# Band attention with a small network on one core: V transposed by DMA instead of TensorE, and GpSimd's low halves issued piece by piece

## What is computed

```
xn = layernorm(x)
Q, K, V = xn Wq + bq, xn Wk + bk, xn Wv + bv            # per head: 1024 x 64
scores = Q K^T where |i - j| <= 64, and 0.0 elsewhere   # zeros stay in the softmax
attention = softmax(scores) V Wo + bo
s = xn Win + bin;  h = relu(s * W1 + b1);  g = sum(h * W2) + b2   # 64 units, 16 inner each
out = x + attention + g Wout + bout
```

## Time and profile before

| | us |
|---|---|
| median of 3 runs | 2201.57 |
| lowest, highest | 2192.87, 2208.58 |
| the profiled execution | 2183.65 |
| its span | 2181.9 |
| mean granted TensorE clock (1.00 is 2.4 GHz) | 0.961 |

### The profile page before, as it was taken

One profiled execution on the slowest core, in us unless ns is written; L12 is line 12 of the kernel. 1 busy time (PEld: TensorE's weight loads), 2 busy tenths in 40 slices (PEclk: granted clock), 3 DMA queues, 4 the chain that ended last, 5 costly groups with the idle time before them and its releaser, 6 DMA issues.

```text
span 2181.9 us, 42699 instructions
## 1 busy us (share of the span) xinstructions
PE 1958.2 (90%) x14211; PEld 1107.1 (51%) x14211; DVE 1824.1 (84%) x4579; ACT 1480.3 (68%) x3961; POOL 1517.1 (70%) x2272
## 2 busy tenths in 40 slices
PE   8768799998999989998899998998989998999985
PEld 4435455554555545554455554554555554555543
DVE  7779687898789887998889888889888898888775
ACT  5767667775767756766667775775757775777753
POOL 3655657877588757867578775686748876687764
PEclk8988899999999999999999999999999999999997
DMA  4454453755366543754356654375444755365534
GB/s 124 118 134 98 97 116 84 174 112 112 69 128 160 101 93 83 164 123 99 81 103 150 136 101 102 80 186 107 87 93 103 173 102 108 78 141 112 117 78 106
DMA packets 610427, 247.04 MB, mean 113 GB/s; under 512 B 547336, under 2 KB 559648, under 8 KB 610208
## 3 DMA queue, kind: packets, MB, share of 16 engines
q1 hardware_dynamic: 610160, 244.30, 50.9%
q10 hardware_dynamic: 48, 0.01, 0.0%
HBM read 84.84 MB, written 25.17 MB: 50 GB/s over the span
## 4 chain that ended last, share of the span: by engine, by line
PE 34%; DVE 26%; POOL 15%; ACT 13%; issue 7%; DMA 5%; SPq 1%; DVEq 0%; ACTq 0%; POOLq 0%
PE ps L1143 17%; POOL probs L388 8%; ACT probs L532 7%; POOL p_lo L401 6%; DVE acc L888 5%; PE ps L1199 5%; PE ps L1158 4%; DVE probs L854 4%; PE ps L1129 4%; DVE v_mean L935 3%; DMA pT_lo<-p_lo 3%; DVE row_l L866 3%; DVE xn L906 2%; ACT p_hi L588 2%; DMA w_kept<-w_split 1%
## 5 line engine op out<-in xcount | busy, mean ns | idle before, releaser
L1143 PE MATMUL ps<-xT_hi,w_split 128*128 128x512 f16 x3072 | 976.8, 382 | 7.9 <-issue 4.4
L388 POOL TENSOR_SCALAR probs<-probs,inv_l,neg_e 128x256 f32<-128x256 f32 x1024 | 589.9, 592 | 283.0 <-DVE neg_e L873 281.5
L401 POOL TENSOR_TENSOR p_lo<-probs,p_hi 128x256 f16<-128x256 f32 x1024 | 678.2, 697 | 39.9 <-ACT p_hi L588 39.9
L1143 PE MATMUL ps<-xT_lo,w_split 128*128 128x512 f16 x1536 | 587.0, 382 | 0.0
L532 ACT ACTIVATE probs<-probs,neg_max 128x256 f32<-128x256 f32 x1024 | 505.7, 498 | 24.4 <-DVE neg_max L861 24.2
L1143 PEld LDWEIGHTS ps<-xT_hi,w_split 128*128 128x128 f16 x3072 | 301.8, 98 | 380.0 <-issue 26.0
L854 DVE CUSTOM_DVE_ANT_0 probs<-ps,mask,unit_s 128x256 f32<-128x256 f32 x1024 | 433.2, 478 | 44.1 <-PE ps L1129 43.6
L888 DVE SCALAR_TENSOR_TENSOR acc<-ps,unit_o,acc 128x512 f32<-128x512 f32 x512 | 356.4, 740 | 30.4 <-PE ps L1158 30.4
L395 POOL TENSOR_TENSOR oT_lo<-o_sum,oT_hi 128x512 f16<-128x512 f32 x128 | 149.0, 1164 | 311.4 <-ACT o_sum L600 311.4
L1158 PE MATMUL ps<-wo_split,oT_hi 128*128 128x512 f16 x1024 | 317.9, 393 | 17.2 <-DVE xT_lo L743 9.2
L588 ACT ACTIVATE p_hi<-probs 128x1024 f16<-128x1024 f32 x256 | 269.5, 1053 | 83.1 <-POOL probs L388 82.8
(11 more groups left out here) (119 smaller groups left out, 2981.4 us busy)
## 6 DMA issues: line engine op xcount, KB each, us to landing
w_split<-w_kept SPq DMA_DIRECT2D x168, 256.0 KB, 3.1
acc<-in_L_attn_x SPq DMA_DIRECT2D x14, 1024.0 KB, 6.4
out_x<-acc SPq DMA_DIRECT2D x14, 1024.0 KB, 5.6
wo_split<-wo_kept SPq DMA_DIRECT2D x56, 256.0 KB, 2.9
w_kept<-w_split SPq DMA_DIRECT2D x24, 256.0 KB, 2.4
pT_hi<-p_hi SPq DMA_TRANSPOSE x256, 3.1
pT_lo<-p_lo SPq DMA_TRANSPOSE x256, 3.3
acc<-in_L_attn_x SPq DMA_DIRECT2D x4, 512.0 KB, 5.7
```

The costliest lines, as they stand in the source:

```text
L388: pool.tensor_scalar(probs[:, h, t], probs[:, h, t], inv_l[:, c:c + 1], neg_e[:, c:c + 1], ALU.mult, ALU.add).then_inc(normed, 1)
L401: last = pool.tensor_tensor(p_split[lo][:, h, t], probs[:, h, t], p_split[hi][:, h, t], ALU.subtract)
L1143: last = pe.matmul(dst[:], w[wp][:, i, c], xT[xp][:, c, half * LINE:half * LINE + LINE], start=(c == 0 and a == 0), stop=(c == KC - 1 and ...
```

## The change

TensorE no longer transposes V: V's high and low half are made from vT, untransposed, and SyncE transposes both by DMA in the next step. ScalarE makes the negative mean of V from the three sums and the value v_back. VectorE makes the low half in the next step, ahead of the second denominators. Each low piece of the weights waits for the piece before it and increments the semaphore itself. In the first eight steps the three stores of split weights and the raw loads stand at the step's beginning. PV half 1 follows K's projection. Scores 0 wait only for the first halves of Q and K. TensorE has new waits for its banks where transposes stood.

```diff
-        v = sb("v", [P, 2, T, 2, 2, D], F16)
+        v_split = [sb(f"v_{part}", [P, N], F16) for part in ("hi", "lo")]
+        v = sb("v", [P, 2, 2, T, 2, D], F16)
...
-        win_raw = sb("win_raw", [P, KC, M])
+        win_raw = p_split[1][:, 0, 0:2].rearrange("p t w -> p (t w)").bitcast(F32).rearrange("p (k m) -> p k m", m=M)
...
@@ SyncE
-                sp.wait_ge((p_hi, p_lo)[part], 4 * j + u + 1)
+                sp.wait_ge(*((p_hi, 4 * j + u + 1), (p_lo, 16 * j + 4 * u + 4))[part])
...
+            def transpose_values(n):
+                if n >= 2:
+                    sp.wait_ge(pv_done, 2 * n - 2)
+                for part, ready in ((hi, v_hi), (lo, v_lo)):
+                    sp.wait_ge(ready, n + 1)
+                    sp.dma_start_transpose(v[:, n % 2, part].rearrange("p t h d -> p t (h d)"), v_split[part][:]) \
+                        .then_inc(v_got, 16)
...
                 def next_weights(i):
-                    if split:
+                    if not split and loads_next:
+                        load_kept(n, i, next_pair)
...
+                if split:
+                    for i in (V_, Q_, K_):
                         keep_weights(n, i, k)
                         if k < PAIRS - 2:
                             load_raw(i, k + 2)
...
                 if attend:
                     transpose_weights(j, 0, 0, hi)
+                    if n <= B * PAIRS:
+                        transpose_values(n - 1)
                     transpose_weights(j, 0, 0, lo)
                     transpose_weights(j, 0, 1, hi)
...
@@ GpSimd
                 def weights_low(half, h):
                     pool.wait_ge(p_hi, 4 * j + 2 * half + h + 1)
-                    for t in tiles_of(half):
-                        last = pool.tensor_tensor(p_split[lo][:, h, t], probs[:, h, t], p_split[hi][:, h, t],
-                                                  ALU.subtract)
-                    last.then_inc(p_lo, 1)
+                    for i, t in enumerate(tiles_of(half)):
+                        if 16 * j + 8 * half + 4 * h + i > 0:
+                            pool.wait_ge(p_lo, 16 * j + 8 * half + 4 * h + i)
+                        pool.tensor_tensor(p_split[lo][:, h, t], probs[:, h, t], p_split[hi][:, h, t],
+                                           ALU.subtract).then_inc(p_lo, 1)
...
@@ ScalarE
                 def value_lines(half):
                     act.wait_ge(v_proj, 2 * n + half + 1)
+                    if half == 0 and n > 0:
+                        act.wait_ge(v_lo, n)
...
-                def values_high(i):
...
+                def value_means():
+                    act.wait_ge(v_in, 2 * n + 2)
+                    if n > 0:
+                        act.wait_ge(v_hi, n)
+                    act.activation(v_parts[:], v_sums[:], ACT.Identity, scale=-1.0 / N, accum_out=v_neg[:]).then_inc(v_stat, 1)
+
+                def values_high():
...
+                    act.activation(v_back[:, n % 2:n % 2 + 1], v_neg[:], ACT.Identity, bias=bias_scaled[:, V_, k:k + 1],
+                                   scale=-1.0).then_inc(v_back_ready, 1)
+                    if n > 0:
+                        act.wait_ge(v_got, 32 * n)
+                    act.activation(v_split[hi][:], vT[:], ACT.Identity, bias=v_neg[:]).then_inc(v_hi, 1)
...
                     value_lines(1)
+                    value_means()
...
+                if proj:
+                    values_high()
                 if attend:
                     weights_high(1, 0)
...
@@ VectorE
-                def centre_values():
...
-                def values_low(i):
...
+                def values_low(m):
+                    dve.wait_ge(v_hi, m + 1)
+                    dve.scalar_tensor_tensor(v_split[lo][:], vT[:], v_neg[:], v_split[hi][:],
+                                             ALU.add, ALU.subtract).then_inc(v_lo, 1)
...
                 if ffn and k == 0:
                     x_low(b, 7)
+                if 0 < n <= B * PAIRS:
+                    values_low(n - 1)
                 if attend:
                     denominators(1)
...
-                row_statistics(3)
...
                 if proj:
                     qk_low(3)
+                row_statistics(3)
...
@@ TensorE
                 def scores(tp):
                     if tp == 0:
+                        pe.wait_ge(qk_lo, 4 * j + 2)
+                    if tp == 1:
                         pe.wait_ge(qk_lo, 4 * j + 4)
...
                 if out_proj:
-                    if n <= B * PAIRS:
-                        pe.wait_ge(v_lo, 2 * n - 1)
+                    if k == 0 and proj:
+                        pe.wait_ge(xT_lo, T * b + 4)
+                    if k == 1 and proj:
+                        pe.wait_ge(ffn_s_in, 2 * b + 2)
+                    if k == 7:
+                        pe.wait_ge(ffn_added, T * b + 6)
+                    pe.wait_ge(v_got, 32 * (o + 1))
                     weigh_values(0)
...
+                if proj:
+                    if attend:
+                        masks_read(1)
+                    project_qk(1)
                 if out_proj:
                     if attend:
                         masks_read(1)
                     else:
                         pe.wait_ge(o_summed, 2 * o)
                     weigh_values(1)
-                if proj:
-                    if attend:
-                        masks_read(1)
-                    project_qk(1)
...
-                if proj:
-                    pe.wait_ge(v_centered, n + 1)
...
-                    transpose_values(0)
...
-                    transpose_values(1)
```

More of the change, by code:

```diff
@@ L102, in band_attention_ffn @@
         SCORE_BANK = ((0, 1), (2, 3), (0, 1), (4, 5))
-        V_BANK, VT_BANK = (6, 1), (6, 7)
+        V_BANK = (6, 1)
         QK_BANK = (7, 2, 2, 3)
@@ L298, in first_kept @@
                     load_kept(n, i, 0)
+                if split:
+                    for i in (V_, Q_, K_):
+                        keep_weights(n, i, k)
+                        if k < PAIRS - 2:
+                            load_raw(i, k + 2)
                 if 2 <= n <= PAIRS + 1:
@@ L601, in weighted_sums @@
                                    scale=1.0 / P_SCALE).then_inc(o_summed, 1)
[L603 to L606 removed]
+                def value_means():
[4 more added lines that the diff above has]
+                def values_high():
+                    act.wait_ge(v_stat, n + 1)
+                    if out_proj:
+                        act.wait_ge(o_summed, 2 * o + 2)
+                    if n < PAIRS:
+                        act.wait_ge(bias_ready, k + 1)
+                    act.activation(v_back[:, n % 2:n % 2 + 1], v_neg[:], ACT.Identity, bias=bias_scaled[:, V_, k:k + 1],
[3 more added lines that the diff above has]
+                    act.activation(v_split[hi][:], vT[:], ACT.Identity, bias=v_neg[:]).then_inc(v_hi, 1)
                 ffn = proj
@@ L931, in qk_low @@
                                              f32(part[hi]), ALU.add, ALU.subtract).then_inc(qk_lo, 1)
-                def centre_values():
-                    dve.wait_ge(v_in, 2 * n + 2)
-                    dve.tensor_tensor(v_mean[:, 0:1], v_sums[:, 0:1], v_sums[:, 1:2], ALU.add).then_inc(v_stat, 1)
-                    dve.wait_ge(v_stat, 3 * n + 1)
-                    dve.tensor_tensor(v_mean[:, 1:2], v_mean[:, 0:1], v_sums[:, 2:3], ALU.add).then_inc(v_stat, 1)
-                    dve.wait_ge(v_stat, 3 * n + 2)
-                    dve.tensor_scalar(v_new[:], v_mean[:, 1:2], 1.0 / N, None, ALU.mult).then_inc(v_stat, 1)
-                    dve.wait_ge(v_stat, 3 * n + 3)
-                    dve.tensor_scalar(vT[:], vT[:], v_new[:], None, ALU.subtract).then_inc(v_centered, 1)
-                def values_low(i):
-                    part = [v[:, n % 2, 4 * i:4 * i + 4, :, p, :].rearrange("p c h d -> p (c h) d") for p in (hi, lo)]
-                    dve.wait_ge(v_hi, 2 * n + i + 1)
-                    dve.tensor_tensor(part[lo], ps[VT_BANK[i]][:].rearrange("p (c d) -> p c d", d=D), part[hi],
-                                      ALU.subtract).then_inc(v_lo, 1)
+                def values_low(m):
+                    dve.wait_ge(v_hi, m + 1)
+                    dve.scalar_tensor_tensor(v_split[lo][:], vT[:], v_neg[:], v_split[hi][:],
+                                             ALU.add, ALU.subtract).then_inc(v_lo, 1)
                 ffn = proj
@@ L1011, in step @@
                     add_network(1)
-                if proj:
-                    centre_values()
                 if ffn and k == 0:
@@ L1182, in network_out @@
                     last.then_inc(ffn_out, 1)
-                def transpose_values(i):
-                    for c in range(4):
-                        last = pe.transpose(ps[VT_BANK[i]][:, c * P:c * P + P],
-                                            vT[:, (4 * i + c) * P:(4 * i + c + 1) * P], ident[:])
-                    last.then_inc(v_T, 1)
                 def weigh_values(half):
@@ L1199, in weigh_values @@
```

(4 more changed lines are left out.)

50 lines of the change are left out of this document (6 added, 44 removed).

## The result

The changed kernel takes 2054.88 us (median of 4 runs, 2046.6 to 2057.42), the kernel before, on the same chip in the same rounds, 2205.07 (2192.87 to 2215.52): ratio 0.9314, interval 0.9258 to 0.9371. The forecast was 2055 us. The profiled execution took 2055.2 us, its span 2053.5. So the time came out as forecast; whether for the forecast's reasons is the question of all that follows.

What follows compares the result with a forecast made beforehand. No engine alone: TensorE's wait for V in k = 6, a four-engine loop in k = 1 to 5, ScalarE's store waits first. Terms sum to -146 us, 2183.65 to 2038; 17.9 for the median gives 2055, range 1995 to 2135.

Steps and rivals of the forecast that it cites:

- first eight steps: Steps that also split and store weights: without ScalarE's waits for stores, 265 us against 310.5, -45 us.
- k = 6, seven: One step per batch, TensorE waiting before V's transposes behind VectorE's sums: seven left, 9.4 us each, -66 us.
- k = 7 and 0, thirteen: Thirteen steps held by TensorE, each losing V's transposes, 0.87 us: -11 us.
- k = 1 to 5, 35: 35 steps held by a loop through four engines: down to 28.5 us, -0.7 each, -24 us.
- part 7: First eight steps: stores and raw loads moved to the step's beginning, their issues hidden, stores landing long before ScalarE needs the place.
- Rival D: The first steps do not follow, held by splitting and the loop: -15 instead of -45, 2085 us, 13%.
- Part 4: All 16 low pieces of a step wait for the one before, 0.10 us each; eight in the loop, +0.8 us.
- parts 2 and 5: 2: V's low half ahead of the second denominators, +0.5 us in the loop; 5: earlier row maxima, at most 0.9 back.
- Parts 3, 6 and 8: 3: two more SyncE transposes; 6: second PV behind K; 8: row statistics, input-weights buffer, added waits; each taken as 0.
- A: Slower, the gaps between pieces used against GpSimd: from 0.56 us a piece, 40 steps eat the 146 us; 7%.
- B: The gaps don't let VectorE in, V's low half kept out to the end of the low pieces: 2117 us, 12%.
- C: 640 DMA transposes instead of 512, the loop's landing 1.23 us later in 40 steps: 2104 us, 13%.

Runs made afterwards that it cites:

- experiment 2: The kernel before with only the stores of split weights and the raw loads moved to the step's beginning: 2187.94 us, ratio 0.9852.
- experiment 3: The changed kernel with the low pieces back to back again, without their waits: 2254.88 us, ratio to the kernel before 1.0163.
- experiment 1: The kernel before with only the pieces changed, each low piece waiting for the one before it: 2112.81 us, ratio 0.9516.
- experiment 4: The changed kernel with V's low half made earlier, between the masks of score pairs 1 and 2: 2013.22 us, ratio to the kernel before 0.9074.
- all but V: The kernel before with pieces, stores first, PV half 1 behind K and the scores' shorter wait, V's old way kept: 2049.8 us, on another chip 2049.05.
- experiments 9 and 10: On one chip, the changed kernel unchanged, 2050.75 us, and beside it all but V, 2049.05 us.
- experiments 7 and 5: 7: changed kernel with V's two DMA transposes done twice, 2048.67 us; 5: changed kernel with PV half 1 ahead of K's projection again, 2049.24 us.
- pairs: The changed kernel with V's low half earlier and a wait only at every second low piece: 1985.54 us, on another chip 1988.85.

## Why the prediction came out right, and where it did not

By its own terms, in the frame in which it was summed:

| term | forecast | measured |
|---|---|---|
| first eight steps | -45 | -41.3 |
| k = 6, seven | -66 | -54.8 |
| k = 7 and 0, thirteen | -11 | -25.1 |
| k = 1 to 5, 35 | -24 | -8.2 |
| start and end | 0 | +1.0 |
| sum | -146 | -128.4 |
| offset to the median | +17.9 | about 0 |

The sum was 17.6 us too large, and the offset of 17.9 us, added for medians above the profiled execution, does not exist in the changed kernel (2055.2 and 2054.88). Two errors of one size cancel: that the median came out at 2055 to the microsecond is luck. The offset was no constant: the kernel before varies from 2160.52 to 2230.38 us over the runs, and its profiled executions differ in k = 1 to 5 (1044.7 in one, 1073.0 in experiment 2, whose edit does not touch these steps). The changed kernel's ten runs lie within 2046.43 to 2057.42. Chance shut-outs would make such a spread, but this is not shown: the kernel of experiment 3, which has the most of them, lies within 2253.87 to 2256.8.

**First eight steps (part 7): right.** Stores first alone brings 31.4 us (experiment 2), and no wait of ScalarE for a store is left. The other 10 us come beside the pieces; which edit brings them is open. Rival D (-15) is out.

**k = 6: right as a place, wrong as to what it takes.** I credited 66 us to V's sums leaving VectorE and nothing to the pieces. The 9.4 us a step were also taken from the longest of the eight waits, 6.19 us, where their mean is 5.25; measured were 7.8, and 33.9 us a step instead of the 32 to 33. The clock that the prediction names behind the 6.19 us of idle time is in the windows of the kernel before: 1.00 in the first of these, 0.50 in the next three, among them the one with the eight transposes of V, and 1.00 again in the last (1.00 is 2.4 GHz).

```profile
1320.60:1322.60 2.00, 0.00 (x0) 0.00 (x0) 1.93 (x4) 0.00 (x0) 0.00 (x0) 1.00 1.20 277
1323.70:1324.90 1.20, 0.00 (x1) 0.04 (x1) 1.20 (x3) 0.00 (x0) 0.00 (x0) 0.50 0.00 0
1324.90:1326.90 2.00, 2.00 (x9) 1.82 (x10) 0.76 (x2) 0.62 (x2) 0.00 (x0) 0.50 0.00 0
1328.50:1330.00 1.50, 1.50 (x9) 0.67 (x8) 0.00 (x0) 0.37 (x1) 0.00 (x0) 0.50 0.00 0
1331.00:1333.00 2.00, 2.00 (x41) 1.77 (x38) 1.97 (x10) 0.00 (x0) 0.00 (x0) 1.00 0.22 83
```

The runs show two sufficient repairs: V by DMA without the waits (236.9 in experiment 3) and the waits without V by DMA (229.6 in experiment 1). With the waits in place V by DMA adds nothing there; it costs 7.8 to 9.9 us.

**Part 4, piece by piece: the step that failed.** "A wait costs 0.10 us [...] +0.8 us" priced the waits as a cost only, and nothing as their return. The cost itself was about right: in experiment 4 four pieces, with three gaps among them, take 2.92 us instead of the 2.55 of the earlier trace rows, 0.12 a gap, and start 0.75 us apart ((2.92 - 0.67) / 3, with 0.67 for one) where I forecast 0.73. But without the waits the changed kernel takes 2254.88 us. So the waits are worth 200 us in the changed kernel, and I had them down as a cost of 0.8 us a step. I priced the stalls of the trace before, where the longest shut-out sat in k = 6, and did not ask who would be the next operation of VectorE to meet twelve queued pieces, once V's sums were gone. It was the network's hidden unit, in k = 1 to 5, for +169 us. I had asked what is late next of TensorE's wait, and not of the shut-out itself.

**k = 1 to 5 (parts 2 and 5): -8 instead of -24.** A step takes 29.6 us (1036.5 / 35) where I forecast 28.5. That some gain is left at all is because the 35 steps had a mean of 29.8 before and not the 29.2 of batch 4 that I reckoned with; batch 4's own five went from 145.8 to 147.9. Two terms were mis-sized. Part 2's +0.5: GpSimd's stretch from the start of the first normalise to the end of the second, averaged over these 35 steps of each trace, is 14.00 us before, 14.50 with the pieces alone, 14.19 in all but V, 14.62 in the changed kernel and 13.67 with V's low half earlier. So V's low half costs 0.95 us where it stands, and what the centring leaves pays for only half of it. Part 5's -0.9 was read from one step: over the whole trace ScalarE waited 24.2 us for row maxima, 0.4 a step, and 13.9 are left, so 0.2 came back. The 1.3 us for the operation's own duration, which the loop's +0.5 uses, is an estimate that no row or run shows; the changed kernel's trace has 1.37 by its median, 1.27 to 1.79. The tile of V's low half in the changed kernel (ns, min/median/max):

```profile
L963 DVE SCALAR_TENSOR_TENSOR v_lo<-vT,v_neg,v_hi x64: 1269/1371/1789, 60.2 to 2017.3; 128x1024 f16<-128x1024 f32 x64
```

Its effect on GpSimd was what I had put too low.

**k = 7 and 0: -25 instead of -11.** V's transposes are there as priced (13.8 us, experiments 9 and 10); another 10.3 come with the pieces (experiment 1), all of them in k = 7 (235.2 to 224.8 us for its seven); VectorE's busy time in those seven falls with them from 217.2 to 194.3 us, stalls that I had not seen there.

**Parts 3, 6 and 8 at nothing: right for 3 and 6**, by experiments 7 and 5. Part 8 and the scores' shorter wait were not tried alone; from pieces only to all but V, k = 1 to 5 fall by 9.1 us, for the scores' wait, the order of PV or the stores; which is open.

**The rivals.** A (the gaps are used against GpSimd) is out: a gap costs 0.12 us and not 0.56, and the waits alone make the kernel faster. B (the gaps don't let VectorE in, 2117) is out: V's low half never took over 1.79 us in the changed kernel, and experiment 3 shows that it is without gaps that VectorE is kept out. C (the DMAs, 2104) is out by experiment 7: with two transposes more again, the time is 2048.67 us.

**The row against the sum.** The small sum took 7.02 us through twelve pieces, and another operation 12.69 through sixteen instructions in experiment 3; with a gap before every piece the same sum took 1.17 at most. The prediction had the first of these and kept it for a rival; it should have carried it into the sum.

## What to carry to other kernels

Where VectorE operations and a queue of GpSimd instructions both work in SBUF, look for short VectorE operations with long durations that end with GpSimd's run, and break the run with a wait of GpSimd on its own semaphore; try every second instruction as well as every one. Removing the operation that is shut out can hand its place to the next, as it did here; and a long VectorE operation belongs where GpSimd is not in the loop. Of a bundle of edits, run each alone and the whole without each: here the part that named the change brought nothing, and a wait in GpSimd's loop over the pieces most of it.

## What the runs showed of the hardware

- VectorE was kept out of its operation through 16 GpSimd instructions that followed each other without a gap, 12.69 us; the operation's median is 0.84. It struck an operation on 128x1 (7.02 us) as well as this one on 128x512. A gap of 0.08 us (81.4 us idle before 1024 pieces in experiment 4), which a wait on the predecessor's semaphore leaves, is enough to let it in: 1.17 us at most for the sum, and no VectorE operation over 1.79 us in the changed kernel. Why most operations get in even without such a gap stays open: before, the median of the sum that took up to 7.02 us was 0.38.
- It works in the other direction too: a piece that met VectorE's 1.51 us operation was held back by 0.97 us (experiment 4).
- The transposes' landing hardly moved with the load on the queues: 3.2 us median in the changed kernel, 3.3 to 3.4 with two more a step (experiment 7).
- TensorE's granted clock was 1.00 when its 6.19 us of idle time before V's transposes began and 0.50 before it ended; the transposes took 1.94 us there and 0.87 at 1.00.
- Not tried: pairs with V's old way. Whether V by DMA pays once its low half stands outside the loop stays open; by the table the earlier place gains 24.2 us in k = 1 to 5 where V by DMA had lost 8.2.
